# A fused attention and feed-forward layer on one core: normalised x transposed by VectorE in quarters of 32 tokens instead of by TensorE

## The reference

```python
x = x + attn(layernorm(x), Wqkv, bqkv, Wo, bo)         # D = 256, one head
x = x + ffn(layernorm(x), gate_w, up_w, down_w, fc1_w, fc2_w, expert_w, ln_gamma, ln_beta)

def layernorm(x, eps=1e-5):
    return (x - mean(x, -1)) / sqrt(var(x, -1) + eps)
def attn(x, Wqkv, bqkv, Wo, bo):
    q, k, v = split(x @ Wqkv + bqkv)                   # (2, 2048, 256) each
    return softmax(q @ k.T / 16) @ v @ Wo + bo
def ffn(h, ...):
    w = sum(top_k(h @ gate_w, 2), -1)
    y = relu(h @ up_w) ** 2 @ down_w + (h @ fc1_w @ expert_w * w) @ fc2_w
    return (y - mean(y)) * rsqrt(var(y) + eps) * ln_gamma + ln_beta
```

## Time and profile before

| | |
|---|---|
| median of 3 runs | 2321.64 us (2321.41 to 2322.28) |
| the profiled execution, its own time | 2322.11 us |
| its span | 2320.3 us |
| TensorE busy | 2307.1 us, 99% |
| VectorE, ScalarE, GpSimd busy | 1578.0, 794.3, 281.0 us |
| chain that ended last | TensorE 92%, VectorE 3%, each other at most 1% |

### The profile page before, as it was taken

One profiled execution on the slowest core, in us unless ns is written; L12 is line 12 of the kernel. 1 busy time (PEld: TensorE's weight loads), 2 busy tenths in 40 slices (PEclk: granted clock), 3 DMA queues, 4 the chain that ended last, 5 costly groups with the idle time before them and its releaser, 6 DMA issues.

```text
span 2320.3 us, 27515 instructions
## 1 busy us (share of the span) xinstructions
PE 2307.1 (99%) x10888; PEld 1939.1 (84%) x10888; DVE 1578.0 (68%) x1772; ACT 794.3 (34%) x885; POOL 281.0 (12%) x550
## 2 busy tenths in 40 slices
PE   9999999999999999999999999999999999999998
PEld 8988988888888878888888888888888888888886
DVE  7787649887989765598763378774249876424548
ACT  4333336666555441522221331213132121223211
POOL 3000000000223200033100023210003220000000
PEclk9999999999999999999999999999999999999999
DMA  8999854532334699978996678898668999666865
GB/s 309 333 359 363 300 193 164 198 122 80 122 120 144 224 314 334 317 276 313 342 308 197 191 275 299 312 335 262 193 219 274 320 331 320 209 193 206 239 209 194
DMA packets 232801, 580.83 MB, mean 250 GB/s; under 512 B 26208, under 2 KB 80096, under 8 KB 232288
## 3 DMA queue, kind: packets, MB, share of 16 engines
q1 hardware_dynamic: 151392, 443.52, 58.1%
q10 hardware_dynamic: 81280, 135.55, 16.0%
HBM read 421.96 MB, written 152.83 MB: 248 GB/s over the span
## 4 chain that ended last, share of the span: by engine, by line
PE 92%; DVE 3%; DMA 1%; SPq 1%; ACT 1%; issue 1%; POOL 1%; ACTq 0%; DVEq 0%; POOLq 0%
PE psum L1116 11%; PE psum L1117 11%; PE psum L1118 11%; PE psum L1095 10%; PE psum L1096 10%; PE psum L1097 10%; PE psum L930 3%; PE psum L928 3%; PE psum L929 3%; PE psum L968 2%; PE psum L998 2%; PE psum L970 2%; PE psum L969 2%; PE psum L1000 2%; PE psum L999 2%; PE psum L948 1%
## 5 line engine op out<-in xcount | busy, mean ns | idle before, releaser
L1751 DVE TENSOR_TENSOR HB<-HB,psum 128x1024 f32<-128x1024 f32 x135 | 163.0, 1217 | 299.1 <-PE psum L1097 299.1
L1972 POOL TENSOR_SCALAR veA<-mvA 128x1 f32<-128x1 f32 x32 | 31.2, 976 | 1269.0 <-DVE mvA L1659 1269.0
L1341 ACT ACTIVATE HB<-HB 128x1024 f32<-128x1024 f32 x64 | 67.8, 1060 | 307.6 <-DVE HB L1751 307.6
L1095 PE MATMUL psum<-XS2h,WR 128*128 128x512 f32 x280 | 109.4, 391 | 1.0 <-DVE XS2l L1457 0.7
L1095 PE MATMUL psum<-XS1h,WR 128*128 128x512 f32 x280 | 109.3, 390 | 0.3 <-DMA WR<-wu_s 0.2
L1095 PE MATMUL psum<-XS0h,WR 128*128 128x512 f32 x280 | 109.1, 390 | 0.0
L1095 PE MATMUL psum<-XS3h,WR 128*128 128x512 f32 x280 | 109.1, 390 | 0.0
L1097 PE MATMUL psum<-XS0h,WR 128*128 128x512 f32 x280 | 109.0, 389 | 0.0
L1096 PE MATMUL psum<-XS1l,WR 128*128 128x512 f32 x280 | 109.0, 389 | 0.0
L1096 PE MATMUL psum<-XS2l,WR 128*128 128x512 f32 x280 | 109.0, 389 | 0.0
L1097 PE MATMUL psum<-XS1h,WR 128*128 128x512 f32 x280 | 109.0, 389 | 0.0
(11 more groups left out here) (402 smaller groups left out, 6616.6 us busy)
## 6 DMA issues: line engine op xcount, KB each, us to landing
WR<-wu_s SPq DMA_DIRECT2D x280, 512.0 KB, 4.3
WR<-wd_s SPq DMA_DIRECT2D x280, 512.0 KB, 4.7
att_s<-ATT ACTq DMA_DIRECT2D x32, 516.0 KB, 3.4
RAW<-in_x_dram SPq DMA_DIRECT2D x32, 512.0 KB, 8.2
RES<-x1b_s SPq DMA_DIRECT2D x128, 128.0 KB, 5.6
out_dram<-ZR ACTq DMA_DIRECT2D x118, 128.0 KB, 5.5
xT_s<-XT SPq DMA_DIRECT2D x24, 512.0 KB, 7.5
HB<-xT_s SPq DMA_DIRECT2D x12, 1024.0 KB, 8.8
```

The costliest lines, as they stand in the source:

```text
L1095: e.matmul(o, w[:, 0, ws], h[:, :, ws], start=kt == 0, stop=False)
L1751: e.tensor_tensor(to, a, src, op=ALU.add).then_inc(*vevac.next(key))
```

## The change

For the blocks u = 2 to 7, x is loaded in another layout: each load `a` brings one quarter of the channels (256) to 32 partitions, so that partition 32a + r holds channels 256a to 256a + 255 of the tokens r, 32 + r, ..., sixteen of them. VectorE's transpose of 32x32 blocks then gives the layout that the products need, with the channels in another order; the rows of the weights for q, k, v and of the gate are loaded in that order too. Mean and variance of a token now lie in four partitions, and a product with a small matrix `FOLD` sums them up. Steps and code, cut to their core:

```diff
+    at(3, "fold_matrix")
     for u in range(2, 8):
         b = 12 * (u - 1)
+        n = 7 if u == 2 else b - 9
         for tt in range(4):
-            if u > 2:
-                at(b - 13, "load_x", u, tt)
-            at(b - 9 + tt, "ln_stats", u, tt)
-        at(b - 6, "ln_rstd", u, 0, 4)
-        for tt in range(4):
-            at(b - 3 + tt // 2, "ln_norm", u, tt)
-        for a in range(4):
-            at(b + 2 * a, "xt_tr", u, a)
-            at(b + 2 * a, xt_out, u, a, b + 2 * a + 1)
+            at(4 if u == 2 else b - 13, "load_x", u, tt)
+            at(n + tt, "x_stats", u, tt)
+        at(n + 4, "x_means", u)
+        at(n + 5, "x_vars", u)
+        at(n + 6, "x_rstd", u)
+        for j in range(4):
+            at(max(n + 8, b) + j // 2, "x_norm", u, j)
+            at(max(n + 8, b) + 1 + j // 2, "x_turn", u, j)
+            at(max(n + 8, b) + 3 + j, "x_parts", u, j)
...
     # TensorE
+        def x_means(u):
+            on.wait_ge(*stats["x", u, 3])
+            on.wait_ge(*zero["fold"])
+            on.wait_ge(*lo["xt", 1, 2])
+            e.matmul(bank(6, 32), FOLD[:, :, :], STX[:, :, :].rearrange("p g (h s) -> p g h s", s=3)[:, :, :, 1],
+                     start=True, stop=True).then_inc(*xt_mm.next(("means", u)))
+        def x_vars(u):
+            on.wait_ge(*stats["dev", u])
+            e.matmul(bank(7, 32), FOLD[:, :, :], DX[:, :, :], start=True, stop=True).then_inc(*xt_mm.next(("vars", u)))
...
     # ScalarE
+        def x_norm(u, j):
+            on.wait_ge(*inv["x", u])
+            for g in range(4 * j, 4 * j + 4):
+                k = e.activation(x_rows(u)[:, g], x_rows(u)[:, g], AF.Identity, bias=NBX[:, g:g + 1], scale=RX[:, g:g + 1])
+        def x_parts(u, a):
+            on.wait_ge(*normed["turn", u, 3])
+            high(XA[u % 2][0][:, 2 * a:2 * a + 2, :], XAT[u % 2][:, 2 * a:2 * a + 2, :], "xt", u, a)
...
     # VectorE
         def ln_norm(t, tt):
-            src = RAW[t % 2][:, tt, :]
+            src = RAW[0][:, tt, :].rearrange("p (q k n) -> p k q n", q=4, k=8)
+            to = RAW[1][:, tt, :].rearrange("p (k q n) -> p k q n", k=8, q=4)
             on.wait_ge(*inv["x", t, tt])
+            on.wait_ge(*(xt_mm[0, 3] if t else lo["e", 3]))
+        def x_stats(u, j):
+            for a in range(4):
+                on.wait_ge(*x_in[u % 2][a][u])
+            for g in range(4 * j, 4 * j + 4):
+                k = e.bn_stats(STX[:, g, :], x_rows(u)[:, g])
+        def x_turn(u, j):
+            on.wait_ge(*v_mm[u - 2, 3])
+            on.wait_ge(*hi["norm", u, j])
+            e.transpose(XAT[u % 2][:, :, 128 * j:128 * j + 128].rearrange("p k (g r) -> p g k r", g=4),
+                        x_rows(u)[:, 4 * j:4 * j + 4].rearrange("p g (k c) -> p g k c", k=8)).then_inc(...)
+        def x_parts(u, a):
+            low(XA[u % 2][1][:, 2 * a:2 * a + 2, :], XAT[u % 2][:, 2 * a:2 * a + 2, :], XA[u % 2][0][:, 2 * a:2 * a + 2, :], "xt", u, a)
...
     # the loads
         def load_x(t, tt):
             if t == 1:
-                on.wait_ge(*lo["e", 3])
+                on.wait_ge(*normed[0, tt])
             elif t > 1:
-                on.wait_ge(*xt_mm[t - 2, 3])
+                on.wait_ge(*raw_done(t - 2))
+                src = x[512 * t:512 * t + 512, 256 * tt:256 * tt + 256].rearrange("(g r) n -> r g n", r=32)
+                e.dma_start(x_rows(t)[32 * tt:32 * tt + 32], src).then_inc(...)
```

More of the change, by code:

```diff
@@ L217, in timetable @@
     do("ln_norm", 0, 3)
+    for tt in range(4):
+        do("load_x", 1, tt)
     do("e2_mm", 0, 1)
@@ L231, in timetable @@
         do("xt_lo", 0, a)
-    for tt in range(4):
-        do("load_x", 2, tt)
     do("e2_mm", 3, 1)
@@ L663, in transformer_layer @@
     RAW = [at(f"RAW{i}", [128, 4, 1024], F32, 176.5 + 16 * i) for i in range(2)]
+    XAT = [at(f"XA{i}t", [128, 8, 512], F32, 128.5 + 32 * i) for i in range(2)]
     OUT = at("OUT", [128, 3, 512], F32, 208.5)
@@ L802, in xt_bank, with wq_parts, wg_parts, raw_done @@
         return 2 * (a % 2) if u == 0 else 6 - 2 * (a % 2)
+    def wq_parts(i, W):
+        return W[:, i].rearrange("p (k q) n -> p k q n", k=2), WQR[:, i].rearrange("p q (k n) -> p k q n", k=2)
+    def wg_parts(W):
+        return W[:, :, 256:264].rearrange("p (k q) n -> p k q n", k=2), GRP[:, :, :].rearrange("p q (k n) -> p k q n", k=2)
+    def raw_done(u):
+        return normed["turn", u, 3] if u > 1 else xt_mm[u, 3] if u else normed[1, 3]
+    def x_rows(u):
+        return RAW[u % 2][:, :, :].rearrange("p t (b n) -> p (t b) n", n=256)
     def v_bank(t, tt):
@@ L1500, in xt_lo, with fold_matrix @@
             low(l, pair(xt_bank(u, a)), h, "xt", u, a)
+        def fold_matrix():
+            on.wait_ge(*const["idn"])
+            e.tensor_reduce(DX[:, :, :].rearrange("p a b -> p (a b)"), idn[:, :].rearrange("p (a r) -> p r a", a=4), axis=AX,
+                            op=ALU.add).then_inc(*zero.next("rows"))
+            on.wait_ge(*zero["rows"])
+            e.tensor_scalar(FOLD[:, :, :], DX[:, :, :].rearrange("p (o a) b -> p o (a b)", o=1).to_broadcast([128, 4, 32]), 0.125,
+                            None, op0=ALU.mult, op1=ALU.bypass).then_inc(*zero.next("fold"))
@@ new lines, in x_stats, with x_means @@
+        def x_stats(u, j):
+            for a in range(4):
+                on.wait_ge(*x_in[u % 2][a][u])
+            if u > 2:
+                on.wait_ge(*xt_mm["means", u - 1])
+            for g in range(4 * j, 4 * j + 4):
+                k = e.bn_stats(STX[:, g, :], x_rows(u)[:, g])
+            k.then_inc(*stats.next(("x", u, j)))
+        def x_means(u):
+            both = STX[:, :, :].rearrange("p g (h s) -> p g h s", s=3)
+            mean = MNX[:, :].rearrange("p (g o) -> p g o", o=1).to_broadcast([128, 16, 2])
+            on.wait_ge(*xt_mm["means", u])
+            if u > 2:
+                on.wait_ge(*inv["dev", u - 1, 3])
+                on.wait_ge(*xt_mm["vars", u - 1])
+            e.tensor_reduce(MNX[:, :], bank(6, 32).rearrange("p (g h) -> p g h", h=2), axis=AX, op=ALU.add).then_inc(*stats.next())
+            on.wait_ge(*stats.now())
+            e.tensor_tensor(DX[:, :, :], both[:, :, :, 1], mean, op=ALU.subtract).then_inc(*stats.next())
+            on.wait_ge(*stats.now())
+            e.tensor_tensor(DX[:, :, :], DX[:, :, :], DX[:, :, :], op=ALU.mult).then_inc(*stats.next())
+            on.wait_ge(*stats.now())
+            e.scalar_tensor_tensor(DX[:, :, :], both[:, :, :, 2], 1.0 / 128.0, DX[:, :, :], op0=ALU.mult,
+                                   op1=ALU.add).then_inc(*stats.next(("dev", u)))
@@ new lines, in x_vars @@
+        def x_vars(u):
+            on.wait_ge(*xt_mm["vars", u])
+            if u > 2:
+                on.wait_ge(*inv["dev", u - 1, 3])
+            e.tensor_reduce(VEX[:, :], bank(7, 32).rearrange("p (g h) -> p g h", h=2), axis=AX, op=ALU.add).then_inc(
+                *stats.next(("var", u)))
+        def x_turn(u, j):
+            on.wait_ge(*v_mm[u - 2, 3])
+            on.wait_ge(*hi["norm", u, j])
+            e.transpose(XAT[u % 2][:, :, 128 * j:128 * j + 128].rearrange("p k (g r) -> p g k r", g=4),
+                        x_rows(u)[:, 4 * j:4 * j + 4].rearrange("p g (k c) -> p g k c", k=8)).then_inc(*normed.next(("turn", u, j)))
@@ L2124, in quad_load @@
             elif b == "qd":
-                on.wait_ge(*xt_mm[6, 3])
+                on.wait_ge(*raw_done(6))
             elif b == "qe":
```

123 lines of the change are left out of this document (80 added, 43 removed).

## The result

The changed kernel takes 2360.66 us (median of 5 runs, 2357.8 to 2362.9), the kernel before in the same rounds 2321.65 us (2321.41 to 2322.38). The ratio is 1.0167, 95% interval 1.0156 to 1.0178: slower by 39 us. Forecast were 2329, with a range of 2305 to 2341. The sign and the place were right; the size was not.

A forecast was written before the change was run, and what follows sets the result against it. The prediction took TensorE, busy 99% of the span, as the bound. Against 2322.1 us its blocks summed to +4.0 - 2.7 + 9.8 - 3.5 = +7.6, 2329.7, or 2329 as a median, range 2305 to 2341.

The forecast's parts named there:

- Small products, +1.7: On TensorE, twelve added products of 32 columns, 0.14 us each, +1.7 us; upper bound 0.3 each, +3.6.
- VectorE's work, 31.1 us a block: VectorE's work per block rises by 2.4 to 31.1 us, where TensorE would need only 33.7; 92% full.
- ScalarE's norms at 0.35: On ScalarE, sixteen normalising pieces of 256 columns per block at 0.35 us each, 5.5 us.
- Block 0 and the start, +4.0: TensorE waits 2.0 at x_means(2) and 1.0 at x_vars; two products 0.3, slower norms 0.6: +4.0 us.
- The loads of x in pieces of 1 KB: same bytes: Loading x in pieces of 1 KB moves the same bytes, so it was costed at nothing.
- Block 1, -2.7: Block 1: -3.5 for the transposes, +0.3 for small products, +0.5 for waiting, together -2.7 us.
- Blocks 2 to 5, the stall of 5.7: TensorE waits at x_means from 21.84 until VectorE's moments at 27.5: 5.7 us, +2.4 per block, +9.8 together.
- The chain of 25.8 us: From ScalarE free at 5.0 through norms, turns, parts, moments and sums: ready 25.8 us after block start, up to 30.
- Rival A: VectorE keeps up, its gaps swallow the turns, no stall above a few tenths: -18.5 us, 2303; chance 0.19.
- Rival B: Transfers set the pace, quad loads land when they did and hold TensorE: 2319, no change; chance 0.27.
- Rival C: At the start, block 1's load or weights land late; 8 us late gives 2337; chance 0.07.
- Rival D: Transposes or moments run slower than their rows; at twice the time +20 us, 2349; chance 0.04.

The follow-up runs named there:

- e16: The changed kernel with x of blocks 2 to 7 loaded in rows of 4 KB instead of 1 KB pieces (wrongly placed numbers); 2353.0 us, ratio 1.0136.
- e1: The changed kernel with 46 transposes of the identity (5.0 us) filling TensorE's wait ahead of x_means for u = 3 to 7; 2360.3 us, ratio 1.0170.
- e13: The changed kernel with loads of the up-projection's quads from the third on cut to 16 of 512 columns; 2361.9 us, ratio 1.0175.
- e18: The changed kernel with x's steps rearranged, x_means and x_vars first at their groups, ScalarE's high parts a separate step, and quads at other groups; 2340.1 us, ratio 1.0081.
- e20: e18 with loads of the up-projection's quads from the third on cut to 16 of 512 columns; 2327.1 us, ratio 1.0023.
- e12: The changed kernel with x's steps, from loads to parts, moved to other groups for room at each link, quads at their old groups; 2347.1 us, ratio 1.0108.
- e11: The changed kernel with the same rearranged steps of x as e12, and quads begun at other groups, at most two away; 2337.7 us, ratio 1.0067.

## Why the prediction was right or wrong

- **Transposes gone, -21.2:** they are gone; not tested by a run of its own, but TensorE's account closes to 0.6 us with it.
- **Small products, +1.7:** 0.13 to 0.45 us each on the path, +3.3. The mean, 0.28, is the upper bound's.
- **VectorE's work, 31.1 us a block:** 31.5. Its terms held: moments 1.40 for four (the next instruction starts after 1.31), turns 1.24, low parts from SBUF 1.22. The lines' answer to the earlier trace rows:

```profile
L1554 DVE BATCH_NORM_STATS2 STX<-RAW 128x6 f32<-128x256 f32 x96 | 33.5, 412 | 5.5 <-DMA RAW<-in_x_dram 5.5
L1583 DVE STREAM_TRANSPOSE XA1t<-RAW 128x1024 f32<-128x1024 f32 x12 | 14.6, 1236 | 4.8 <-ACT RAW L1205 4.8
```

- **ScalarE's norms at 0.35:** they start 0.5 apart (eight in 4.05), 8.2 us a block in place of 5.5. The forecast read 0.57 for 512 columns and let the time fall with the width; the pieces of 512 in the timeline above start 0.52 apart (three in 1.67), so half the width saves next to nothing. GpSimd's eight instructions, 8 us by the forecast and hidden, take 5.2 to 8.5 us to the last that a norm needs. They were hidden but for block 2, where they began 5.1 us before the block and not 8.7, and ended together with ScalarE's store issues.
- **Block 0 and the start, +4.0:** block 1 began 7.0 us later (76.1 against 69.1). The wait fell on another instruction, the v product behind block 1's last low part (4.1 us, and 2.4 for the slow group), because VectorE stood 3.0 us for block 2's x. "The loads of x in pieces of 1 KB: same bytes" was the failed step here: the loads take 11.7 us to land (median of 106 to 254 us) where e16's rows of 4 KB take 8.0. The weights' pieces of 1 and 2 KB, with the gate's of 64 bytes among them, show in the window 20 to 30 us, before and then after:

```profile
20.00:30.00 10.00, 10.00 (x61) 8.45 (x60) 6.65 (x9) 4.62 (x6) 2.43 (x9) 1.00 1.02 414
```

```profile
20.00:30.00 10.00, 10.00 (x61) 8.43 (x60) 6.69 (x8) 4.44 (x6) 2.63 (x9) 1.00 1.11 259
```

  The Trainium skill, "DMA: Bandwidth & Descriptors", section "Why small descriptors are slow (HBM only)", gives a fixed 3 cycles a packet beside one cycle for 32 bytes; an estimate from that is 35 cycles for 1 KB instead of 32, 9%. What these rows show is much more, so the measurement decides. Whether it comes from the pieces' length or from the 32 partitions that a load fills now stays open, as no run has one without the other.
- **Block 1, -2.7:** missed. `x_means` of u = 3 waited 3.1 and `x_vars` 1.0, where the forecast had 0.5; the block took 38.9 us, 1.9 longer than before.
- **Blocks 2 to 5, the stall of 5.7:** the mechanism and the place were right, the size was not. TensorE arrived 21.9 to 23.3 us after the block's start (21.84 forecast). The moments were ready after 33.3, 27.1, 29.2 and 32.8 us, mean 30.6, against 27.5 forecast and 30 at worst. The step that failed is "I take 27.5, 2 us above the old mean for 4.6 us of turns": it let more than half of the turns fall into VectorE's idle gaps. Windows from each block's start to the moment when these moments are ready, first of the kernel before, then of the changed one, show that none did:

```profile
106.08:132.70 26.62, 26.62 (x141) 22.59 (x140) 19.44 (x30) 10.82 (x14) 0.00 (x0) 1.00 1.01 369
143.05:167.70 24.65, 24.65 (x127) 20.77 (x126) 18.82 (x30) 10.20 (x13) 0.00 (x0) 1.00 1.02 393
180.03:206.20 26.17, 26.17 (x137) 22.13 (x136) 17.86 (x28) 12.36 (x15) 0.00 (x0) 1.00 0.99 366
217.00:241.40 24.40, 24.40 (x126) 20.56 (x125) 19.37 (x28) 11.97 (x12) 0.00 (x0) 1.00 0.97 358
```

```profile
114.98:148.26 33.28, 22.24 (x98) 17.76 (x96) 25.36 (x39) 19.51 (x31) 5.18 (x15) 0.89 0.95 338
163.39:190.47 27.08, 21.93 (x98) 17.83 (x96) 22.01 (x34) 19.64 (x31) 2.12 (x9) 0.97 0.93 318
205.03:234.21 29.18, 21.93 (x98) 17.83 (x96) 22.08 (x35) 21.26 (x32) 2.33 (x10) 0.93 0.90 323
249.06:281.77 32.71, 21.93 (x98) 17.84 (x96) 24.24 (x35) 18.62 (x27) 0.54 (x3) 0.88 0.94 322
```

  VectorE's work in this stretch (the third of the busy times, DVE) rises from a mean of 18.9 to 23.4 us, by as much as the turns take, and it stands idle 7.1 us where it stood 6.6. Already its work alone is longer than the 21.84 us after which TensorE asks. Its queue stands for `v_out` until the block's start, so a stall of none, the forecast's floor, was out of reach in this order. The chain of 25.8 us, by which the forecast checked itself, was right at its start and too short behind it. ScalarE's first norm came 2.1 to 4.0 us after the block's start (5.0 forecast); from there to the end of the last turn passed 9.8 to 13.2 us (7.4), and from there to the last moments 13.5 to 20.8 (13.4). In between stood slower norms, in block 2 a quad's high parts (3.5), in blocks 2 and 5 a quad's low part (2.2), in blocks 4 and 5 high parts of x queued behind a quad's (2.0 and 2.4), and in block 5 a load of x (2.4). Waits in blocks 2 to 5 add up to 33.4 us, not 22.8. A term that the sum left out altogether is the clock: v groups at half speed, 2.5 us each after waits of 4 us and more, 12.7 us in TensorE's account; what is known of their real cost is e1's.
- **Block 6, -3.5:** block 6 took 33.4 us (296.7 to 330.1) against 37.0: right.
- **Rival A** (VectorE keeps up) was wrong in the changed order. **Rival B** (the quads' loads) was wrong in it too (e13), but right of e18 for 13 us (e20). **Rival C** did not occur: block 1's transposes began at 48.7 us, before at 48.5. **Rival D** did not: the operations cost what their rows said.

Sum of the difference to the forecast, 30.4 us: stalls in blocks 2 to 5 10.6, block 1's 3.6, slow groups 12.7, small products 1.6; the remaining 1.9 is the start and the 1.0 for `qk_out`. This sum says where TensorE's time lies and not what each item would return: in e1, 4.6 us of slow groups returned nothing. What another order of x's steps returned is 13.5 us with the quads as they were (e12) and 23 with the quads moved too (e11).

What stays open: what the best order would give, and what the clock costs by itself. e20 with fewer bytes still has 12.9 us of waits and a clock below 1.00 in three of five windows from 76 to 270 us, and none of them was taken further.

## What to carry to other kernels

When the bound engine is made to wait for one that is 90% full, spare time per period does not price the wait. What prices it is the work that stands in that engine's queue from the start of the period to the answer, against the moment at which the bound engine asks: here 23.4 us against 21.84, before any idle time. Do not let new work fill old gaps on paper, unless what the engine waits for in them stays where it was; here 6.6 us of gaps became 7.1 with 4.6 us more work. Where its queue also stands for the bound engine itself (here `v_out`), the two take turns and the loss repeats in every block. Put the asking instruction as far behind the work, and the answer as far ahead of the rest of its queue, as buffers allow. And when an experiment shows a resource not to bind, that holds for that order only.
